# Most TensorE products issued as two matmuls of 64 columns, in a two-layer cross-attention and FFN kernel

## The reference, cut to what matters

```
x = x + attention0(layernorm(x), ctx)     # q = x Wq, k = ctx Wk, v = ctx Wv; softmax(q k' / 8) v; times Wo, plus bo
x = x + ffn0(layernorm(x))                # silu(x wg') * (x wu') times wd', weights of integers / 127
x = x + attention1(layernorm(x), ctx)
x = x + ffn1(layernorm(x))                # rows and weights quantised to 8-bit integers, one 256 x 256 product
```

## Time and profile before

| | us |
|---|---|
| median of 3 runs | 1649.87 (1648.95 to 1650.41) |
| the profiled execution | 1653.73 |
| its span, first to last instruction | 1651.7 |
| PE busy | 1600.0 |
| ACT busy | 1382.6 |
| DVE busy | 1363.5 |
| POOL busy | 1267.5 |

### The profile page before, as it was taken

How to read it: one execution, slowest core, us unless ns; L and a number is a source line. 1 busy time by engine, 2 the same in 40 slices (tenths; PEclk the granted TensorE clock), 3 DMA queues, 4 the chain that set the end, 5 groups by cost and what they waited for, 6 DMA issues and landing times.

```text
span 1651.7 us, 52223 instructions
## 1 busy us (share of the span) xinstructions
PE 1600.0 (97%) x16114; PEld 1314.1 (80%) x16114; DVE 1363.5 (83%) x3519; ACT 1382.6 (84%) x5665; POOL 1267.5 (77%) x1888
## 2 busy tenths in 40 slices
PE   7999988999999999999999999999999999999995
PEld 4665566888888888888888888888888888888883
DVE  5667667888888888888888877888888888888885
ACT  5665588888888898988888888889999999999993
POOL 4200077898898988988988988788888888888883
PEclk9999999999999999999999999999999999999997
DMA  8955689777777787787777887699898889888994
GB/s 249 346 211 215 244 191 179 165 164 178 170 174 172 168 175 176 162 177 173 163 176 165 173 165 166 144 177 193 195 195 185 188 191 197 186 189 191 196 187 86
DMA packets 732994, 305.43 MB, mean 185 GB/s; under 512 B 621424, under 2 KB 718608, under 8 KB 730832
## 3 DMA queue, kind: packets, MB, share of 16 engines
q1 hardware_dynamic: 731616, 299.39, 80.1%
q0 software_dynamic: 1264, 4.72, 0.8%
HBM read 87.72 MB, written 65.54 MB: 93 GB/s over the span
## 4 chain that ended last, share of the span: by engine, by line
PE 77%; POOL 5%; issue 3%; DVE 1%; DMA 1%; SPq 1%; ACT 0%; POOLq 0%; ACTq 0%
PE psum L1087 19%; PE psum L304 18%; PE psum L1074 13%; PE psum L1102 11%; PE psum L1111 10%; PE psum L1118 5%; POOL pr L1486 2%; PE psum L293 1%; POOL p L1489 1%; POOL p L1493 1%; PE psum L1124 1%; DMA pT<-p 0%; POOL rs L354 0%; DMA x2T<-x 0%; POOL hT_l L1476 0%
## 5 line engine op out<-in xcount | busy, mean ns | idle before, releaser
L1220 ACT ACTIVATE ex<-psum,nmax 128x77 f32<-128x77 f32 x2048 | 638.8, 334 | 44.5 <-DVE nmax L1341 38.0
L1220 ACT ACTIVATION_READ_ACCUMULATOR ex<-psum,nmax 128x1 f32 x2048 | 439.8, 215 | 0.0
L1493 POOL TENSOR_TENSOR p<-pr,p 128x308 f16<-128x308 f32 x512 | 405.0, 791 | 38.5
L1486 POOL TENSOR_TENSOR pr<-ex,rden 128x308 f32<-128x308 f32 x512 | 381.2, 744 | 65.3 <-DVE rden L1346 64.6
L304 PE MATMUL psum<-xT,wq_h 128*128 128x256 f16 x2048 | 349.8, 273 | 0.0
L1341 DVE TENSOR_REDUCE nmax<-psum 128x4 f32<-128x308 f32 x512 | 242.0, 473 | 82.3 <-PE psum L1074 77.3
L1087 PE MATMUL psum<-wo_h,oT_h 128*128 128x256 f16 x1024 | 281.0, 274 | 10.9 <-DVE oT_l L323 10.8
L1087 PE MATMUL psum<-wo_l,oT_h 128*128 128x256 f16 x1024 | 280.8, 274 | 0.0
L1087 PE MATMUL psum<-wo_h,oT_l 128*128 128x256 f16 x1024 | 280.7, 274 | 0.0
L304 PE MATMUL psum<-xT,wq_l 128*128 128x256 f16 x1024 | 279.6, 273 | 0.0
L1074 PE MATMUL psum<-kb,qT_h 128*128 128x154 f16 x2048 | 259.7, 232 | 8.3 <-DVE qT_l L326 4.7
(11 more groups left out here) (153 smaller groups left out, 3312.9 us busy)
## 6 DMA issues: line engine op xcount, KB each, us to landing
keys<-ks SPq DMA_DIRECT2D x16, 1232.0 KB, 5.2
kb<-keys SPq DMA_DIRECT2D x256, 77.0 KB, 2.7
vb<-vals SPq DMA_DIRECT2D x128, 154.0 KB
vals<-vs SPq DMA_DIRECT2D x64, 256.0 KB, 3.0
x_pair<-in_x_dram SPq DMA_DIRECT2D x32, 256.0 KB, 3.2
pT<-p SPq DMA_TRANSPOSE x512, 3.2
x_res<-in_x_dram SPq DMA_DIRECT2D x32, 256.0 KB, 3.0
mid_x<-y SPq DMA_DIRECT2D x32, 256.0 KB, 2.4
```

The lines of the kernel that those rows point to most:

```text
L1220: last = act.activation(ex[i][:, t, b, :], SC[:, t, b * NK:(b + 1) * NK], ACT.Exp, bias=nmax[i][:, t, b:b + 1], accum_out=den[i][:, t, b:b ...
L1486: pool.tensor_tensor(pr[:, t, :, :], ex[i][:, t, :, :], r, ALU.mult).then_inc(s_p, 1)
L1493: pool.tensor_tensor(d[:, t, 1, :, 0:NK], pr[:, t, :, :], d[:, t, 0, :, 0:NK], ALU.subtract).then_inc(s_pl, 1)
```

## The change

A new helper `product` issues a matmul either as it was or as a pair: the same moving operand, once with the first 64 columns of the stationary tile into PSUM rows 0 to 63, once with the other 64 columns into rows 64 to 127. The arithmetic is the same.

- Layer 1: all of its scores, queries (those that are issued in its bodies), `quantised`, and `project` except in slot 1, become pairs.
- Layer 0: scores and queries in slots 0, 1 and 3, `project` in slots 0, 1 and 3, and `gate_up` for all chunks but chunk 1 (which is issued in slot 2) become pairs. `down` stays as it was in both of its places (slot 2).
- Transposes, and the two `queries` at the end of the first part, stay full width.
- Layer 1's items of Wq and Wo are no longer late: all eight items are prepared in the first part, at eight places, and the loads, roundings, low parts and the wait of bodies 1, 2, 3 and 31 are gone. POOL issues all eight loads, in a new order and with new waits.

```diff
-        qo_items, late_items = qo_items[:4], qo_items[4:]
         NQO, NT = len(qo_items), len(turned)
-        qo_raw = [raw[:, 0, :], raw[:, 1, :], qo_land[:, 0, :], qo_land[:, 1, :]]
+        qo_raw = 2 * [qo_land[:, 0, :], qo_land[:, 1, :], raw[:, 0, :], raw[:, 1, :]]
...
+        def product(pe, o, w, x, halved, **flags):
+
+            if not halved:
+                return pe.matmul(o, w, x, **flags)
+            for b in range(2):
+                last = pe.matmul(o[b * DH:(b + 1) * DH], w[:, b * DH:(b + 1) * DH], x, **flags)
+            return last
...
-                    last = pe.matmul(oo, ww[:, k, w], xT[par][:, :, part, k, :], start=(q == 0),
-                                     stop=(q == len(terms) - 1))
+                    last = product(pe, oo, ww[:, k, w], xT[par][:, :, part, k, :], halved, start=(q == 0),
+                                   stop=(q == len(terms) - 1))
...
-        QO_AT = {(1, 24): 0, (1, 50): 1, (2, 24): 2, (3, 43): 3}
+        QO_AT = {(0, 43): 0, (0, 47): 1, (1, 6): 2, (1, 24): 3, (1, 50): 4, (2, 6): 5, (2, 24): 6, (3, 43): 7}
...
                 def load_qo(k):
-                    if k < 2:
-                        pool.wait_ge(s_kl, k + 5)
+                    if k >= 4:
+
+                        pool.wait_ge(s_wl, k - 3)
+                    elif k >= 2:
+                        pool.wait_ge(s_kl, k + 3)
...
-                for n in range(NT):
-                    paced(n)
-                    load_ints(n)
-                    if n < NQO:
-                        load_qo(n)
+                load_qo(0)
+                load_qo(1)
+                paced(KVL + 6)
+                load_qo(2)
+                load_qo(3)
+                for j in range(NT):
+                    paced(KVL + 12 + 5 * j)
+                    load_ints(j)
+                for k in range(4, 8):
+                    load_qo(k)
...
-                        if like == 1:
-                            load_late(u)
...
+                def paired(u, lay):
+
+                    return lay[0] == 1 or u != 2
...
-                            last = pe.matmul(o, w[:, a, ts], kb[u // 2][:, :, part, u % 2 * PPU + a, :], start=(q == 0),
-                                             stop=(q == 2))
+                            last = product(pe, o, w[:, a, ts], kb[u // 2][:, :, part, u % 2 * PPU + a, :], halved,
+                                           start=(q == 0), stop=(q == 2))
...
-                                last = pe.matmul(OA[:, t, :], oo[:, a, ts], ww[:, m, :], start=first,
+                                last = product(pe, OA[:, t, :], oo[:, a, ts], ww[:, m, :], u != (1 if l == 1 else 2),
...
-                            last = pe.matmul(oo, w[:, k, c * P:(c + 1) * P], x2T[:, :, part, k, :], start=(q == 0),
-                                             stop=(q == len(terms) - 1))
+                            last = product(pe, oo, w[:, k, c * P:(c + 1) * P], x2T[:, :, part, k, :], c != 1,
+                                           start=(q == 0), stop=(q == len(terms) - 1))
...
-                        last = pe.matmul(o[:, 0, :], qiT[:, k, t * P:(t + 1) * P], rhs_q[:, k, :], start=(k == 0),
-                                         stop=(k == KT - 1))
+                        last = product(pe, o[:, 0, :], qiT[:, k, t * P:(t + 1) * P], rhs_q[:, k, :], True,
+                                       start=(k == 0), stop=(k == KT - 1))
...
-                    if like == B - 1:
-
-                        pe.wait_ge(s_ll, len(late_items))
...
-                        if like == 2:
-                            _, hi, lo, scale = late_items[u]
-                            act.wait_ge(s_late[u], 16)
-                            act.activation(hi, late_raw[:, u, :], ACT.Copy, scale=scale).then_inc(s_lh, 1)
...
-                        if like == 3:
-                            _, hi, lo, scale = late_items[u]
-                            dve.wait_ge(s_lh, u + 1)
-                            dve.scalar_tensor_tensor(out=lo, in0=late_raw[:, u, :], scalar=scale,
-                                                     in1=hi, op0=ALU.mult,
-                                                     op1=ALU.subtract).then_inc(s_ll, 1)
```

More of the change, by code:

```diff
@@ L164, in xattn_ffn_kernel @@
         s_rr = sem("s_rr")
-        s_ro = [sem(f"s_ro{i}") for i in range(4)]
+        s_ro = [sem(f"s_ro{i}") for i in range(8)]
         s_int = sem("s_int")
@@ L295, in turn, with queries @@
             return last
-        def queries(pe, u, l, par, o):
+        def product(pe, o, w, x, halved, **flags):
[4 more added lines that the diff above has]
+            return last
+        def queries(pe, u, l, par, o, halved):
             for a in range(PPU):
@@ L481, in load_qo, with paced @@
                     pool.dma_start(d, src).then_inc(s_ro[k], 16)
-                def paced(n):
-                    pool.wait_ge(s_kvf, RING + KVL + 6 * n)
-                for n in range(NT):
-                    paced(n)
-                    load_ints(n)
-                    if n < NQO:
-                        load_qo(n)
+                def paced(j):
+                    pool.wait_ge(s_kvf, RING + j)
+                load_qo(0)
[8 more added lines that the diff above has]
+                    load_qo(k)
                 pool.dma_start(rhs_raw[:, :].rearrange("p (t d) -> p t d", d=D),
@@ L792, in _ @@
                             pe.wait_ge(s_wte, 2 * NT)
-                            queries(pe, 0, 0, 0, RG[0])
+                            queries(pe, 0, 0, 0, RG[0], False)
                         if (i, j) == (3, 27):
-                            queries(pe, 1, 0, 0, RG[1])
+                            queries(pe, 1, 0, 0, RG[1], False)
         early.close()
-        late_raw = sb("late_raw", [P, len(late_items), INNER], F32)
         x_res = sb("x_res", [P, QT, D], F32)
@@ L834, in xattn_ffn_kernel @@
         yo = sb("yo", [P, QT, D], F32)
-        s_late = [sem(f"s_late{k}") for k in range(len(late_items))]
-        s_lh, s_ll = sem("s_lh"), sem("s_ll")
         s_vb = [sem(f"s_vb{g}") for g in range(2)]
@@ L974, in turn_second_rows @@
                                            x216[:, :, :, :].rearrange("p t r d -> p (t r d)")).then_inc(s_x2d, 16)
[L976 to L980, removed]
                 sp.sem_inc(s_y, 16)
@@ L1063, in _, with scores @@
             def _(pe):
-                def scores(k, u, t, k_need):
+                def paired(u, lay):
+                    return lay[0] == 1 or u != 2
+                def scores(k, u, t, k_need, halved):
                     if t == 0:
@@ L1086, in project @@
                                 first = u == 0 and t == 0 and a == 0 and q == 0
-                                last = pe.matmul(OA[:, t, :], oo[:, a, ts], ww[:, m, :], start=first,
-                                                 stop=(u == UNITS - 1 and a == PPU - 1 and q == 2),
-                                                 skip_group_check=True)
+                                last = product(pe, OA[:, t, :], oo[:, a, ts], ww[:, m, :], u != (1 if l == 1 else 2),
+                                               start=first, stop=(u == UNITS - 1 and a == PPU - 1 and q == 2),
+                                               skip_group_check=True)
                     if u == UNITS - 1:
@@ L1146, in body @@
                         if lay[0] is not None:
-                            scores(n + u, u, 0, 32 * (h + 1))
+                            scores(n + u, u, 0, 32 * (h + 1), paired(u, lay))
                         if u == 2 and lay[-3] == 0:
@@ L1158, in body @@
                                 pe.wait_ge(s_xl, h + 3 - B)
-                            queries(pe, (u + 2) % UNITS, lay[(u + 2) // UNITS], (like + (u + 2) // UNITS) % 2, bank("q", u))
+                            queries(pe, (u + 2) % UNITS, lay[(u + 2) // UNITS], (like + (u + 2) // UNITS) % 2, bank("q", u), paired(u, lay))
                         if u == 2 and lay[-2] == 1:
@@ L1164, in body @@
                         if lay[0] is not None:
-                            scores(n + u, u, 1, 0)
+                            scores(n + u, u, 1, 0, paired(u, lay))
                         if u == 0 and lay[-3] == 0:
```

## The result

| | before | after |
|---|---|---|
| median, us | 1649.42 (4 runs, 1648.95 to 1650.41) | 1631.31 (4 runs, 1629.97 to 1632.44) |
| ratio | | 0.9889, 95% interval 0.9873 to 0.9904 |
| the profiled execution, us | 1653.73 | 1632.44 |

The kernel is 18.1 us faster. (The profile of before lies 4 us above its median, that of after 1; the two spans, 1651.7 and 1630.6, thus overstate the gain.)

A forecast was written before the change was run, and what follows sets the result against it. PE was taken as the bound, with work at every moment. 12.3 + 1 + 8.1 + 3 - 0.9 = 23.5 us off the profiled 1653.7 gave 1630.2, or 1626 as a median; range 1603 to 1658.

The forecast's parts named there:

- rival 2: Both layers: chains on the other engines take nearly all of PE's gain, leaving 1634 to 1642 us; chance 0.10.
- A passage costs 0.23: Around `weigh_values`: going from full width to 64 columns and back loses 0.23 us; 191 passages go, 44 us.
- A pair costs what a full product costs: All halved products: nothing added, pairs at 0.108 us for 256 columns and, at the lower end taken, 0.068 for 154.
- Rival 3: Halved score products: pairs of 154 columns bound by loads or issue, 0.108 us each, +108 us, 1712; chance 0.18.
- rival 5: Every halved product: longer by one exposed load of 0.03 us, 270 us in all, 1875; chance 0.02.
- Layer 1's slot 0 gives its passage back: Layer 1, slot 0's `project`: already waits for `oT_l` on DVE's chain from `x1`, so the whole 0.23 us is lost.
- Layer 1's slot 3 gives 0.20 back: Layer 1, slot 3's `project`: `oT_l` follows slot 2's `nmax` through DVE's final FFN additions, so 0.20 us is given back.
- Rival 1: DVE and ACT, slowed by POOL: a new rhythm clears the chains and all 44 us stay, 1604; chance 0.10.
- Layer 0's slot 1 waits 0.25: Layer 0, slot 1's `project`: new wait of 0.25 us for `oT_l`, so 0.44 of 0.69 us per body is kept.
- The ends were taken as free: Gains per body applied to 28 bodies of layer 0 and 31 of layer 1, plus 1 us for the first four.
- The late items: Stretch 236 to 312: moving layer 1's late items saves 3 us of waits and costs 0.9 in the first part.
- Instruction supply: PE's queue: four instructions per halved product, one every 17 ns in scores; 24 ns seen, left as part of the doubt.

The follow-up runs named there:

- e2: The changed kernel with pairs kept in layer 0 only, layer 1 at full width: 1639.68 us, ratio 0.9941 to the kernel before.
- e1: The changed kernel with every product at full width again, so only the move of the late items is left: 1646.38 us, ratio 0.998 to before.
- e3: The changed kernel with pairs kept in layer 1 only, layer 0 at full width: 1639.21 us, ratio 0.994 to the kernel before.
- e4: The changed kernel with only the queries as pairs, in every slot, and all other products at full width: 1700.63 us, ratio 1.0311 to before.
- e6: The changed kernel with layer 1's second normalisation statistics taken over 128 of the 256 features (values differ from the reference): 1623.0 us, ratio 0.9849 to before.
- e5: The changed kernel with layer 0's slot 2 in pairs too, including `down`, `gate_up(1)` and layer 0's last `project`: 1668.9 us, ratio 1.0125 to before.
- e11: e1 with PE's loops alone running over four bodies a turn instead of two: 1691.85 us, ratio 1.0257 to the kernel before.
- e10: e1 with the loops of all engines running over four bodies a turn instead of two: 1699.23 us, ratio 1.0292 to the kernel before.
- e12: e1 with the loops of ACT and DVE alone running over four bodies a turn instead of two: 1665.07 us, ratio 1.0084 to the kernel before.

## Why the prediction was right, and where it was off

| term | forecast | measured |
|---|---|---|
| layer 0 | 12.3 + 1 | 6.7 (e2 against e1) |
| layer 1 | 8.1 | 7.2 (e3 against e1) |
| late items, less their cost in the first part | 3 - 0.9 = 2.1 | 2.4 (e1) |
| sum | 23.5 | 16.3; the whole change 18.1 |

(The parts come from different sets of runs, each with its own spread of a us or so, and need not add up.)

By the time alone 1631 is not far from rival 2, whose lower end was 1634. The bodies decide: they kept 0.33 and 0.38 us, where rival 2 left one passage of 0.23. That layer 1's 7.2 lies so near the forecast is luck: a gain in slot 3 that I had not foreseen made up for losses at the ends, as told below.

- **A passage costs 0.23: right.** In after, `weigh_values` to the next group takes 656 ns instead of 778, and `project` to `weigh_values` 1310 instead of 1400; the slots 0 and 3 of layer 0, which have no wait, are shorter by 0.22 and 0.20. e4, which puts the gap where there was none, is 0.227 per slot.
- **A pair costs what a full product costs: right.** Queries take 1307 ns in either form, six scores 410. Rival 3 (pairs of 154 columns at 0.108) is refuted by every scores group in slots without a wait, and so is rival 5, which has each pair longer by a load. By the Trainium skill, "TensorE: Matmul & The Clock Gate" (LDWEIGHTS), the two loads of a pair were 107 ns, one after the other, as an estimate; six pairs in 410 ns leave 68 for both. The measurement decides: there is no such bound here.
- **Layer 1's slot 0 gives its passage back: right.** `scores` to `project` waits 0.32, the slot is 21 ns longer than before, and e6 shows the chain.
- **Layer 1's slot 3 gives 0.20 back: wrong.** It kept all of its 223 ns. The step said that `oT_l` there follows slot 2's `nmax` and the additions of the FFN at a fixed distance, with 0.03 of slack. The distance did not stay: the last of these additions, `yo`, takes 1.06 us in before and 0.69 in after. The rows are of body 41, first before, then after:

```profile
1209.47 0.75 POOL L1493 TENSOR_TENSOR p<-pr,p 128x308 f16<-128x308 f32 x1
1209.70 1.06 DVE L1445 TENSOR_TENSOR yo<-ya,x 128x512 f32<-128x512 f32 x1
...
1197.78 0.69 DVE L1446 TENSOR_TENSOR yo<-ya,x 128x512 f32<-128x512 f32 x1
1197.84 1.24 POOL L1488 TENSOR_TENSOR p<-pr,p 128x308 f16<-128x308 f32 x1
```

  In before POOL's product had begun when `yo` did; in after `yo` is 0.06 ahead, and POOL's product is the long one. So `oT_l` ends 0.22 before PE comes for it (1199.46 against 1199.68). What the step would have given can be seen in one body: in body 36 of after, `yo` lasts 1.02, `project` begins 0.055 after `oT_l`, and slot 3 takes 4287 ns, 0.19 more than the 4094 of bodies 38 to 59, where `yo` lasts 0.69. The arithmetic held, but the lengths of DVE's instructions were taken as fixed, and they hang on how DVE and POOL meet. A steady body gained 0.38 and not 0.26.
- **Rival 1 in small.** This is its new rhythm, in one chain of three; the waits of slot 0 and of layer 0's slot 1 came. Of what it says of POOL's neighbours, before's trace shows it for DVE in `yo`, but not for ACT: an exponential (`ex`, 77 columns) lasts 0.33 us on average whether POOL is busy beside it throughout or not at all.
- **Layer 0's slot 1 waits 0.25: 0.20 came.** The last scores group has 588 ns on average (536 to 639) instead of 410, and `project` starts 0.024 late in itself. But slot 2 is 106 ns longer than before, and no step of mine looked there: in every second body `gate_up(0)` begins 0.10 to 0.18 later than in the others (761 to 838 ns after `weigh_values`, against 657), and `down(1)` waits 0.05 on average. Kept 0.33 instead of 0.44.
- **The ends were taken as free: wrong.** I multiplied by all 28 and 31 bodies and added 1 for the first four. Relative to e1's profile, after's bodies 0 to 4 lose 1.0, bodies 28 to 40 gain 0.8 in all, and the last two lose 1.3; only the loops gain at the steady rate. One wait of PE named `issue`, in code outside the loops, is enough for the first 1.0: it ends at 237.5 in after and is 1.68 us long, in e1 0.34. The ends and slot 2 make layer 0's shortfall of 6.6; in layer 1 the unforeseen slot 3 made up for it.
- **The late items: right on balance.** In 236 to 312 the wait for `oT_l` of the earlier trace rows went from 4.2 to 0.5, and one of 3.4 for the turned rows (`x2T`) went too, but one of 3.4 for `qT_l` came. Bodies 0 to 4 take 6.4 us less in e1's profile than in before's; the medians, 2.4 apart, leave no room for that much, so a part of it, and perhaps of the 4.2, belongs to before's profiled execution, which lies 4 above its median. The first part ended 2.4 us later than before and not 0.9. What can be pinned on the change is the 0.8 at each of the two places shown above, instead of the 0.23 of the earlier trace rows. The rest is less firm: 0.7 stood already before the first tile, and in the profiles of the experiments with this same first part it ends anywhere from 0.1 us before before's to 2.4 after it.

```profile
PE psum L301 <- DVE qT_l L333: 3.4, 1, 3.4
...
PE psum L301 <- DVE oT_l L330: 0.5, 1, 0.5
```

- **Instruction supply.** I asked only whether PE could issue more instructions per us, and it can: pairs of 154 columns are four instructions in 68 ns. I did not ask whether the loop's turn still fits. It does, at 1724 instructions, and by little: with one more slot in pairs, the better-looking e5, this change would have been 19 us slower than before.

## What to carry to other kernels

Count the changes of width of the stationary tile: on a full PE each passage to 64 columns and back was 0.22 to 0.23 us, and issuing everything in pairs of 64 columns cost nothing in itself, even at 154 moving columns. Before making a hardware loop's turn longer, count its instructions on each engine and look whether the fetch queue falls silent inside the loop; if it doesn't, each jump costs several us, the stall and in most cases some time at the low clock after it. When pricing a chain that PE will run into, do not take the lengths of DVE's instructions as fixed: look which of them POOL's lengthen now, and whether they will still meet. Price the bodies at a pipeline's ends apart from the steady ones.

## What the runs showed of the hardware that I had not expected

- A loop that does not stay in PE's instruction memory stalls for 2 to 4 us at each jump, in work that is otherwise the same (e11, 14.2 us in five waits; 4.5 lost per jump in all), while its fetches go on as they do in code without a loop (in e5 a packet of q8 every 5 us on average inside layer 0's loop, every 7 behind it). For ACT and DVE it was 2 to 5 us a jump of layer 0 (e10, e12).
- A stall of 2.5 to 3.2 us was mostly followed by a stretch at half the clock (0.50), which cost 1.5 us more (e11, layer 1).
- One and the same addition on DVE (`yo`, 128x512) lasts 0.69 or 1.06 us, by whether it begins just before a product of POOL's or during one.
- The price of a change of width depends on neither the rows (77 or 128) nor the kind of product: 0.09 to 0.10 on each change, and 0.01 to 0.03 at the second product after it.
- From 128 rows to 77 within 64 columns costs nothing (0.11 from the last pair of `project` to `weigh_values`).
